# First layer: a plain pause before the transposes of the next chunk's rows becomes a rest until the next scan step

## The chip, the core and the metric

The kernel runs as one program on one core of a Trainium2 chip, in float32 throughout. The metric is the device time of one execution in microseconds (us). TensorE is called PE here, VectorE DVE, ScalarE ACT, GpSimd POOL, and SP is the engine that issues most DMAs.

## The reference

Four blocks with residual sums run over `x` of 4 sequences of 2048 rows, 256 wide: a time-mixing block with a gated linear recurrence, a mixture of 2 shared and 16 routed experts (these two are the first layer of the kernel), a selective state-space block, and a dropless mixture of 2 x 32 experts. The part that matters here is the head of the first block:

```python
x = x + _L0_attn_ref(_layernorm(x), ...)
x = x + _L0_ffn_ref(_layernorm(x), ...)
...
def _L0_attn_ref(x, ...):
    h = rms_norm(x, ln1_w)
    xx = jnp.pad(h[:, :-1], ((0, 0), (1, 0), (0, 0))) - h
    xr = h + xx * mu_r            # likewise xk, xv, xw, xg
    r, k, v = xr @ Wr, xk @ Wk, xv @ Wv
    g = silu(xg @ Wg)
    decay = exp(-exp(w0 + tanh(xw @ wA) @ wB))
    # per head: o_t = r_t (S + u k_t v_t);  S = decay_t S + k_t v_t
    o = group_norm(o) * gn_w + gn_b
    x = x + (o * g) @ Wo
    x = x + gelu(rms_norm(x, ln2_w) @ ffn_w1) @ ffn_w2
```

## The kernel before, in words

The first layer (`layer0_phase`) takes the 8192 rows in 16 chunks of 512. Each chunk's recurrence is a scan of 32 steps, one per pair of a half of the channels (2) and a value column (16). In every step POOL multiplies keys and values (L876), DVE scans along time (L885) and multiplies the states by the receptance (L891), and every fourth step PE sums four products (L907).

All other work is written as Python generators that are advanced while the instructions of the scan are recorded, so a fixed order of instructions per engine comes out; each engine then runs its own list in order and waits on semaphores. In step `g`, `background.pull()` advances five streams, each by its rate: `before(c + 1)`, which prepares the next chunk, at 1.3 advances per step, the head norms at 1.5, `attention_out` and `expert_inputs` at 3. A stream's unused part of an advance is carried on, so at 1.3 a stream is advanced once in most steps and twice in every third or fourth one. After that `block_work` (the experts of chunk `c - 2` and the feed-forward of chunk `c - 1`) is advanced until PE has been given about 4800 columns in the step; what the streams put on PE counts in this sum. A `yield` ends an advance, so what stands behind it is recorded at the next advance, which may lie in the same step. `rest(steps)` yields until the step counter has moved on by so many steps, at most three times for each:

```python
            until = now[0] + steps
            for _ in range(3 * steps):
                if now[0] >= until:
                    break
                yield
```

`before(c)` goes: statistics of the rows `xa` (`normalise`, DVE and POOL), ACT scaling them into `ha` in two pairs of 128 rows with a `yield` between them (`scaled`, L359), then `transposed`: for each half of the channels four PE transposes into one PSUM bank (L369) and ACT moving that bank to `hT` (L377). Then come, each with its own yields, the mixes (DVE L428), decay (PE, ACT L475, L477), keys and receptance (ACT L441), values (ACT L501), and the gate (PE, ACT L517, DVE L520), and the bonus (PE with `of_head`, DVE L530). The PE results of all these streams, of W_up of the experts and of the feed-forward's first product go into a ring of three PSUM banks, `G`; `claim` takes the next bank that is not held, and the matmul waits until the one who read it last is done.

Others named below: the head norm (`head_norm`) is a PE matmul with `centre`, a square on ACT (L553), a PE matmul with `same_head`, then Ln and Exp on ACT (L561, L563), for which ACT loads another table (L559), and two DVE multiplies (L566, L569). The experts go W_up on PE, Gelu on ACT (L791), a multiply by the gate on POOL (L802) and W_down on PE (L783), which runs three experts behind W_up. The feed-forward does the same with `w1`, Gelu (L666) and `w2` (L658). The gates come from a router matmul on PE, a softmax and top-4 on ACT and DVE (up to L728), a PE transpose (L733), a copy on ACT (L741), and two DMAs that spread them. `experts_out` (DVE L815) adds an expert sum to the rows and so frees the two banks of W_down.

Steps are counted from 0 to 31 in the scan of the chunk before the one that is prepared.

Of the kernel before, what the change touches and what calls it, by code (L numbers as in the profile page):

```python
# [210 lines left out]
def layer0_phase(nc, psum, consts, I, L, sems, x_in, x_out, second_layer):  # L211
# [6 lines left out]
    with ExitStack() as st, ExitStack() as scanning:  # L218
# [92 lines left out]
        def rest(steps):  # L311
# [6 lines that stand above are left out]
# [33 lines left out]
        def scaled(dst, src, scale, bias):  # L351

            for t in range(TL):
                if t == TL // 2:
                    yield
                if bias is None:
                    m = act.mark(nc.scalar.activation(dst[:, t, :], src[:, t, :], ACT.Copy, scale=scale[:, t:t + 1]))
                else:
                    m = act.mark(nc.scalar.activation(dst[:, t, :], src[:, t, :], ACT.Identity, scale=scale[:, t:t + 1], bias=bias[:, t:t + 1]))  # L359
            return m  # L360
# [33 lines left out]
        def before(c):  # L394
# [15 lines left out]
            yield  # L410
            act.after(m, m_done.get(("mixed", c - 1)))
            m = m_done["xa free", c] = yield from scaled(ha, xa, roots[:, TL:], shift[0])
            yield
            act.after(m_halo)
            marks = yield from transposed(ha, lambda kb: hT[:, kb, 1:C + 1], m, lambda kb: cols["ln1_w"][:, kb:kb + 1])
            yield
# [515 lines left out]
        def stages(c):  # L932

            def prepare():
                main, chain, inputs, ahead = [], [], [], [first] if c == 0 else []
                if c >= 1:
                    main.append(block_work(c - 2 if c >= 2 else None, c - 1))
                    chain.append(attention_out(c - 1))
                    inputs.append(expert_inputs(c - 1))
                if c + 1 < NCH:  # L940
                    ahead.append(before(c + 1))
                return main, chain, inputs, ahead, [head_norm(c, 0)]
            return prepare

        last = NCH - 1

        first = before(0)
        Background((1, [first])).drain(until=lambda: is_done(("ready", 0)))
        load_xa(1)
# [1136 lines left out]
```

How the kernel before makes its waits and increments, by code:

```python
    def after(self, *marks):  # L49
        for m in marks:
            if m is None or m.body != self.body or self.waited.get(m.lane, 0) >= m.ordinal:
                continue
            self.waited[m.lane] = m.ordinal
            self.engine.wait_ge(m.lane.sem, m.lane.base + m.ordinal)
# [6 lines left out]
    def finish(self):  # L63
        assert self.count < LANE_STEP
        if self.count:
            self.engine.wait_ge(self.sem, self.base + self.count)
        self.engine.sem_inc(self.sem, LANE_STEP - self.count)
# [14 lines left out]
    def begin(self, index):  # L83
        self.bodies += 1
        for lane in self.all:
            lane.begin(index * LANE_STEP + 1, self.bodies)
        for lane in self.all:
            for other in self.all:
                if other is not lane:
                    lane.engine.wait_ge(other.sem, other.base)
        self.sp.engine.sem_inc(self.sp.pause, 1)
# [117 lines left out]
def layer0_phase(nc, psum, consts, I, L, sems, x_in, x_out, second_layer):  # L211
# [77 lines left out]
        dve.mark(nc.vector.memset(carry[:, :], 0.0))  # L289
        dve.mark(nc.vector.memset(hT[:, :, C], 0.0))
        dve.mark(nc.vector.memset(kv[:, :, 0], 0.0))
        for i in range(2):
            m_first = dve.mark(nc.vector.memset(decay[i][:, :, 0], 1.0))
        dve.engine.wait_ge(s_load, loaded_first)
        dve.after(m_first)
        dve.mark(nc.vector.tensor_scalar(col_pack[:, len(A_COLS):, :], col_pack[:, len(A_COLS):, :], 0.5, None, ALU.mult))
```

## Time and profile before

| | |
|---|---|
| median of 3 runs | 4985.46 us (4985.34 to 4995.43) |
| profiled execution, its own time | 4976.51 us |
| its span from the first to the last instruction | 4974.7 us |
| mean granted TensorE clock | 0.935 |
| busy: PE, DVE, POOL, ACT | 88%, 77%, 61%, 51% |

The first layer takes about the first 2200 us of the span. A busy PE is not PE at its peak, and the sum of busy times of one engine says little on which engine makes the others wait; that is read from the waits and from the engines' instructions in order of time.

### The profile page before, as it was taken

To read this page: it belongs to the slowest core of one execution; us is meant where nothing else is said; L and a number is where in the kernel's file an instruction comes from. 1 tells how busy PE (TensorE), PEld (TensorE's weight loads), DVE (VectorE), ACT (ScalarE), POOL (GpSimd) and SP (SyncE) were. 2 spreads that over 40 slices of the span, in tenths; PEclk is the share of its full clock that TensorE was granted. 3 is DMA by queue.
4 is the path that set the end of the run, shared out by engine and by line. 5 is a ranking of instruction groups with operands and counts; after the bars stand their busy time and mean duration, and the time that the engine had idled before them with its cause. 6 is when DMAs were issued, how large, how long until landed. Compare 5 with 4: busy or idle time off the path is not lost.

```text
span 4974.7 us, 58244 instructions
## 1 busy us (share of the span) xinstructions
PE 4357.1 (88%) x18832; PEld 2868.4 (58%) x18832; DVE 3827.0 (77%) x6152; ACT 2521.3 (51%) x4753; POOL 3045.1 (61%) x1956
## 2 busy tenths in 40 slices
PE   5789999999999999998988889998988888489994
PEld 1355555555555555565655655555555555378883
DVE  6897888878777887884168888888888888645677
ACT  1244333433433343333567777777777776245552
POOL 3455554545545455553167888888888888745552
PEclk7899999999999999999989999999999998699997
DMA  4233332333333233332121121112221111486787
GB/s 143 80 106 107 104 102 85 109 106 102 106 104 104 84 108 106 98 110 84 45 85 55 71 71 64 64 65 74 77 84 65 70 65 61 162 240 205 255 279 279
DMA packets 302509, 545.46 MB, mean 110 GB/s; under 512 B 30592, under 2 KB 146560, under 8 KB 293248
## 3 DMA queue, kind: packets, MB, share of 16 engines
q1 hardware_dynamic: 274560, 466.08, 29.0%
q0 software_dynamic: 27648, 75.67, 4.2%
q8 instruction: 153, 2.51, 0.2%
q14 instruction: 148, 1.21, 0.1%
HBM read 422.71 MB, written 118.92 MB: 109 GB/s over the span
## 4 chain that ended last, share of the span: by engine, by line
PE 59%; DVE 18%; ACT 10%; POOL 6%; issue 4%; DMA 2%; SPq 0%; DVEq 0%; another core or an unknown queue 0%; POOLq 0%; ACTq 0%
PE psum L207 23%; PE psum L783 8%; PE psum L1891 5%; DVE c_hs L1426 5%; PE psum L658 5%; POOL c_dbx L1408 4%; PE psum L1150 4%; PE psum L1442 3%; DVE a_S L885 3%; PE psum L1914 3%; PE psum L1198 3%; DVE a_prod L891 2%; PE psum L907 2%; ACT psum L1415 2%; PE psum L1876 1%
## 5 line engine op out<-in xcount | busy, mean ns | idle before, releaser
L1408 POOL TENSOR_TENSOR c_dbx<-c_dtx,c_Brep 128x1024 f32<-128x1024 f32 x512 | 1203.0, 2365 | 266.6 <-DVE c_hs L1426 211.3
L876 POOL TENSOR_TENSOR a_kv<-a_rk,a_kv 128x512 f32<-128x512 f32 x512 | 813.5, 1601 | 387.4 <-DMA a_kv<-v_rows 387.4
L1426 DVE TENSOR_TENSOR_SCAN c_hs<-psum,c_carry,c_dbx 128x512 f32<-128x512 f32 x768 | 934.8, 1264 | 148.7 <-ACT psum L1415 115.9
L802 POOL TENSOR_TENSOR a_hid_e<-a_hid_e,a_g_rep 128x512 f32<-128x512 f32 x256 | 386.8, 1513 | 823.8 <-ACT a_hid_e L791 646.9
L885 DVE TENSOR_TENSOR_SCAN a_S<-a_decay,a_carry,a_kv 128x513 f32<-128x513 f32 x512 | 792.0, 1547 | 103.0 <-POOL a_kv L876 99.0
L1415 ACT ACTIVATE psum<-c_dt,c_cols 128x512 f32<-128x512 f32 x1024 | 694.1, 687 | 296.7 <-DVE c_hs L1426 288.1
L1442 PE MATMUL psum<-ident,c_hs 128*128 128x128 f32 x4096 | 656.6, 299 | 152.8 <-DVE c_hs L1426 146.5
L1442 PEld LDWEIGHTS psum<-ident,c_hs 128*128 128x128 f32 x4096 | 521.7, 153 | 410.5 <-DVE c_hs L1426 239.8
L891 DVE TENSOR_TENSOR a_prod<-a_rk,a_S 128x512 f32<-128x512 f32 x512 | 580.9, 1135 | 78.8 <-PE psum L907 78.8
L783 PE MATMUL psum<-a_W_down,a_hid_e 128*128 128x256 f32 x2304 | 550.9, 385 | 62.1 <-DVE a_carry L883 35.5
L207 PE MATMUL psum<-a_xT,a_W_up 128*128 128x512 f32 x1152 | 561.1, 617 | 26.2 <-ACT a_hid_e L791 15.2
L783 PEld LDWEIGHTS psum<-a_W_down,a_hid_e 128*128 128x128 f32 x2304 | 436.0, 192 | 226.6 <-issue 79.8
L1804 POOL DMA_INDIRECT results<-d_ys,d_to_row x320 | 312.0, 975 | 241.5 <-issue 145.3
L207 PEld LDWEIGHTS psum<-a_xT,a_W_up 128*128 128x128 f32 x1152 | 217.6, 195 | 268.5 <-issue 208.5
L1426 DVE TENSOR_TENSOR_SCAN c_hs<-psum,c_dbx 128x512 f32<-128x512 f32 x256 | 296.6, 1207 | 68.3 <-ACT psum L1415 49.8
L791 ACT ACTIVATE a_hid_e<-psum 128x512 f32<-128x512 f32 x288 | 171.1, 594 | 323.6 <-PE psum L207 322.9
L1891 PE MATMUL psum<-d_w,d_xT 128*128 x1280 | 331.3, 382 | 0.4 <-ACT d_xT L1879 0.2
L1365 POOL DMA_INDIRECT sorted_rows<-route_xn,route_to_row x256 | 263.0, 1027 | 64.8 <-issue 46.9
L1198 PE MATMUL psum<-c_xs,c_W_dt 128*128 128x512 f32 x512 | 255.5, 625 | 23.6 <-ACT c_dt L1223 21.0
L207 PE MATMUL psum<-a_xT,a_w 128*128 128x256 f32 x1024 | 240.8, 384 | 10.9 <-ACT a_decay L475 7.8
L658 PE MATMUL psum<-a_w,a_hid_f 128*128 128x256 f32 x1024 | 244.6, 382 | 1.5 <-ACT a_hid_f L666 0.3
L1150 PE MATMUL psum<-c_pre,c_taps 128*128 128x512 f32 x512 | 242.5, 596 | 0.5 <-ACT c_pre L1143 0.4
(263 smaller groups left out, 6890.9 us busy)
## 6 DMA issues: line engine op xcount, KB each, us to landing
a_kv<-v_rows SPq DMA_DIRECT2D x512, 256.0 KB
a_g_rep<-g_rows SPq DMA_DIRECT2D x256, 256.0 KB, 4.0
c_Brep<-b_rows SPq DMA_DIRECT2D x64, 1024.0 KB
d_xs<-sorted_rows SPq DMA_DIRECT2D x320, 128.5 KB
d_w<-results SPq DMA_DIRECT2D x64, 512.0 KB, 11.4
d_w<-in_d_experts SPq DMA_DIRECT2D x32, 768.0 KB
sorted_rows<-d_zeros SPq DMA_DIRECT2D x66, 128.5 KB, 11.3
a_xa<-in_L_attn_x SPq DMA_DIRECT2D x16, 512.0 KB, 4.6
```

The lines of the kernel that those rows point to most:

```text
L207: last = nc.tensor.matmul(out, lhsT, rhs, start=(n == 0), stop=(n == len(pairs) - 1))
L658: m_down = nc.tensor.matmul(sums[:, t * D:(t + 1) * D], hid_f[:, r, s * HALF + t * P:s * HALF + (t + 1) * P], w2[:, 2 * (f - 1) + s, :], s ...
L783: m_down = nc.tensor.matmul(banks[t // 2][1][:, (t % 2) * D:(t % 2 + 1) * D], hid_e[:, r, t * P:(t + 1) * P], W_down[:, q, :], start=(q == ...
L876: m_kv[g] = pool.mark(nc.gpsimd.tensor_tensor(kv[:, g % NV, 1:C + 1], rk[slot][:, 1, hb, :], kv[:, g % NV, 1:C + 1], ALU.mult))
L885: m_scan[q] = dve.mark(nc.vector.tensor_tensor_scan(S[:, q % NS, :], decay[cq % 2][:, hb, :], kv[:, q % NV, :], carry[:, sq_:sq_ + 1], ALU ...
L891: m_prod[q] = dve.mark(nc.vector.tensor_tensor(prod[:, q % NP, :], rk[cq % 2][:, 0, sq_ // DK, :], S[:, q % NS, 0:C], ALU.mult))
L1150: m = nc.tensor.matmul(bank, taps[:, e, j, :], pre[:, e, j:j + C], start=(j == 0), stop=(j == KC - 1))
L1408: m_dbx[g] = m_dbx[g + 1] = pool.mark(nc.gpsimd.tensor_tensor(dbx[:, r:r + 2, :], dtx[slot][:, e, :].unsqueeze(1).broadcast_to([P, 2, C]), ...
L1415: m_da[g] = act.mark(nc.scalar.activation(psum[:, DA + g % ND, :], dt[slot][:, e, :], ACT.Exp, scale=A[:, e, n:n + 1]))
L1426: m_scan[q] = dve.mark(nc.vector.tensor_tensor_scan(hs[:, q % NR, :], psum[:, DA + q % ND, :], dbx[:, q % NX, :], first, ALU.mult, ALU.add))
L1442: last = nc.tensor.matmul(psum[:, YB + e % 2, t * P:(t + 1) * P], hs[:, q % NR, t * P:(t + 1) * P], ident[:, :], is_transpose=True, start= ...
L1891: m = nc.tensor.matmul(bank[:, 0:2 * P], xT[:, q % N3, kb * P:(kb + 1) * P], w[:, bass.ds(at_w[q] + kb * 2 * P, 2 * P)], start=(kb == 0), ...
```

## The change

The pause between the last scaling by ACT and the first transpose is a rest of one step in place of a plain yield.

```diff
@@ -410,7 +410,7 @@
             yield
             act.after(m, m_done.get(("mixed", c - 1)))
             m = m_done["xa free", c] = yield from scaled(ha, xa, roots[:, TL:], shift[0])
-            yield
+            yield from rest(1)
             act.after(m_halo)
             marks = yield from transposed(ha, lambda kb: hT[:, kb, 1:C + 1], m, lambda kb: cols["ln1_w"][:, kb:kb + 1])
             yield
```

The numbers of instructions stay the same on every engine; their order changes, and more than the one line shows, since every later yield of `before(c)`, the columns given to `block_work`, and the phase in which the stream enters the next chunk move with it. In the order of before, chunks 3 to 15 are all alike: scaling in steps 5 and 6, transposes in steps 6 and 7. In the changed order they come in two kinds that alternate. For odd chunks (3, 5 to 15) the scaling stays in steps 5 and 6, the transposes come in steps 7 and 8, and the last instruction of `before` moves from step 29 to step 31. For even chunks (4 to 14) the scaling comes in steps 4 and 5 and the transposes stay in steps 6 and 7. Three places show it.

The first is PE around the transposes of chunk 7 (`a_ha` are its scaled rows, `a_sq` is the head norm's square). Before:

```order
L783 MATMUL psum<-a_W_down,a_hid_e 128x256 x4
L207 MATMUL psum<-a_sq,a_same_head 128x512
L369 MATMUL psum<-ident,a_ha 128x128 x4
L207 MATMUL psum<-a_xT,a_W_up 128x512 x2
L907 MATMUL psum<-a_prod,a_to_value 32x512 x4
L369 MATMUL psum<-ident,a_ha 128x128 x4
```

and now:

```order
L207 MATMUL psum<-a_sq,a_same_head 128x512
L783 MATMUL psum<-a_W_down,a_hid_e 128x256 x4
L207 MATMUL psum<-a_xT,a_W_up 128x512 x2
L907 MATMUL psum<-a_prod,a_to_value 32x512 x4
L369 MATMUL psum<-ident,a_ha 128x128 x4
L783 MATMUL psum<-a_W_down,a_hid_e 128x256 x4
```

The first transposes stood right behind the matmul with `same_head`; now a W_down, a W_up and the scan's sums stand between.

The second is a place that the diff does not mention: the head norm of the first half of the channels, in steps 20 to 24, and what PE and ACT have around it. PE before, around the second values matmul (`a_Wv`):

```order
L207 MATMUL psum<-a_xm,a_Wv 128x512 x2
L658 MATMUL psum<-a_w,a_hid_f 128x256 x4
L907 MATMUL psum<-a_prod,a_to_value 32x512 x4
L207 MATMUL psum<-a_sq,a_same_head 128x512
L783 MATMUL psum<-a_W_down,a_hid_e 128x256 x4
L207 MATMUL psum<-a_xT,a_W_up 128x512 x2
L207 MATMUL psum<-a_xm,a_Wg 128x512 x2
```

PE now, for an odd chunk (first fence) and for an even one:

```order
L207 MATMUL psum<-a_xm,a_Wv 128x512 x2
L207 MATMUL psum<-a_sq,a_same_head 128x512
L658 MATMUL psum<-a_w,a_hid_f 128x256 x4
L207 MATMUL psum<-a_xT,a_W_up 128x512 x2
L783 MATMUL psum<-a_W_down,a_hid_e 128x256 x4
L207 MATMUL psum<-a_xm,a_Wg 128x512 x2
```

```order
L207 MATMUL psum<-a_xm,a_Wg 128x512 x2
L207 MATMUL psum<-a_sq,a_same_head 128x512
L783 MATMUL psum<-a_W_down,a_hid_e 128x256 x4
L207 MATMUL psum<-a_xT,a_W_up 128x512 x2
L207 MATMUL psum<-a_xm,a_Wg 128x512 x2
L783 MATMUL psum<-a_W_down,a_hid_e 128x256 x4
```

ACT now, for the same odd chunk and the same even one:

```order
L501 COPY a_rv<-psum 128x512 x2
L559 ACT_TABLE_LOAD
L561 ACTIVATE a_sq<-psum,eps 128x512
L563 ACTIVATE a_sq<-a_sq 128x512
L666 ACT_TABLE_LOAD
L666 ACTIVATE a_hid_f<-psum 128x512
L791 ACTIVATE a_hid_e<-psum 128x512 x2
L517 ACTIVATE a_gate<-psum 128x512
```

```order
L561 ACTIVATE a_sq<-psum,eps 128x512
L563 ACTIVATE a_sq<-a_sq 128x512
L517 ACT_TABLE_LOAD
L517 ACTIVATE a_gate<-psum 128x512
L791 ACT_TABLE_LOAD
L791 ACTIVATE a_hid_e<-psum 128x512 x2
```

For the odd chunk `same_head` stands right behind the values matmul and `w2` right behind `same_head`, while the last Gelu of the feed-forward (L666) has moved behind Ln and Exp on ACT. For the even chunk the first gate matmul stands ahead of `same_head`, the tanh of the gate (L517) stands between Exp and the Gelu (L791), and a second table load stands between tanh and Gelu.

The third is PE at the start of a chunk, from the router matmul on. Before:

```order
L207 MATMUL psum<-a_W_router,a_xT 128x16 x8
L907 MATMUL psum<-a_prod,a_to_value 32x512 x4
L207 MATMUL psum<-a_xT,a_W_up 128x512 x8
L783 MATMUL psum<-a_W_down,a_hid_e 128x256 x4
L733 MATMUL psum<-ident,a_gates 16x128 x4
L207 MATMUL psum<-a_xT,a_W_up 128x512 x2
L783 MATMUL psum<-a_W_down,a_hid_e 128x256 x4
L207 MATMUL psum<-a_xT,a_W_up 128x512 x2
L783 MATMUL psum<-a_W_down,a_hid_e 128x256 x4
```

and now:

```order
L207 MATMUL psum<-a_W_router,a_xT 128x16 x8
L783 MATMUL psum<-a_W_down,a_hid_e 128x256 x4
L207 MATMUL psum<-a_xT,a_W_up 128x512 x8
L907 MATMUL psum<-a_prod,a_to_value 32x512 x4
L733 MATMUL psum<-ident,a_gates 16x128 x4
L783 MATMUL psum<-a_W_down,a_hid_e 128x256 x4
L207 MATMUL psum<-a_xT,a_W_up 128x512 x2
L783 MATMUL psum<-a_W_down,a_hid_e 128x256 x4
L207 MATMUL psum<-a_xT,a_W_up 128x512 x2
L783 MATMUL psum<-a_W_down,a_hid_e 128x256 x4
```

The last W_down of the previous chunk's experts comes behind the router, and the transposes of the gates come ahead of the first W_down of the next experts and not behind it.

## Rows read from the trace of the kernel before

**Rows 1.** busy time in one chunk of layer 0: length, PE, PEld, DVE, ACT, POOL, clock, DMA.

```profile
746.24:889.19 142.95, 133.81 (x520) 82.93 (x520) 118.74 (x146) 55.50 (x92) 76.30 (x49) 0.99 0.31 102
```

**Rows 2.** waits of PE over layer 0: total us, times, longest.

```profile
PE psum L369 <- ACT a_ha L359: 47.6, 15, 13.7
PE psum L783 <- DVE a_carry L883: 35.5, 13, 3.1
...
PE psum L783 <- POOL a_hid_e L802: 26.6, 15, 2.2
```

**Rows 3.** PE in order of time, near 746 us: start, length, instruction, [idle before].

```profile
742.70 1.02 PE L207 MATMUL psum<-a_sq,a_same_head 128*128 128x512 f32 x2
746.24 0.63 PE L369 MATMUL psum<-ident,a_ha 128*128 128x128 f32 x4 [2.51 <-ACT a_ha L359]
748.05 3.36 PE L207 MATMUL psum<-a_xT,a_W_up 128*128 128x512 f32 x4 [1.19 <-ACT a_hid_e L791]
```

**Rows 4.** ACT in order of time, the same place.

```profile
743.76 0.69 ACT L561 ACTIVATE a_sq<-psum,eps 128x512 f32<-128x512 f32 x1 [0.94 <-PE psum L207]
744.48 0.63 ACT L563 ACTIVATE a_sq<-a_sq 128x512 f32<-128x512 f32 x1
745.01 1.08 ACT L359 ACTIVATE a_ha<-a_xa,a_shift,a_roots 128x256 f32<-128x256 f32 x2
746.11 1.28 ACT L791 ACT_TABLE_LOAD   x1
```

**Rows 5.** PE in order of time, from a chunk's last router matmul into the next chunk.

```profile
850.27 1.85 PE L207 MATMUL psum<-a_W_router,a_xT 128*128 128x16 f32 x16
852.06 1.06 PE L907 MATMUL psum<-a_prod,a_to_value 128*32 128x512 f32 x8
853.05 7.13 PE L207 MATMUL psum<-a_xT,a_W_up 128*128 128x512 f32 x16
863.14 1.97 PE L783 MATMUL psum<-a_W_down,a_hid_e 128*128 128x256 f32 x8 [2.96 <-DVE a_carry L883]
...
872.44 1.99 PE L783 MATMUL psum<-a_W_down,a_hid_e 128*128 128x256 f32 x8 [1.73 <-POOL a_hid_e L802]
```

**Rows 6.** DVE in order of time, the same place.

```profile
861.58 0.22 DVE L728 TENSOR_TENSOR a_gates<-a_gates,a_router_total 128x64 f32<-128x64 f32 x1
861.72 1.28 DVE L815 TENSOR_TENSOR a_xb<-a_xb,psum 128x512 f32<-128x512 f32 x2
...
863.26 1.29 DVE L885 TENSOR_TENSOR_SCAN a_S<-a_decay,a_carry,a_kv 128x513 f32<-128x513 f32 x1
864.46 0.67 DVE L891 TENSOR_TENSOR a_prod<-a_rk,a_S 128x512 f32<-128x512 f32 x1
```

**Rows 7.** PE at the same place one chunk earlier.

```profile
717.20 3.17 PE L783 MATMUL psum<-a_W_down,a_hid_e 128*128 128x256 f32 x8 [3.11 <-DVE a_carry L883]
720.16 1.06 PE L733 MATMUL psum<-ident,a_gates 128*16 128x128 f32 x4
```

**Rows 8.** POOL in order of time, that earlier place.

```profile
727.17 2.49 POOL L802 TENSOR_TENSOR a_hid_e<-a_hid_e,a_g_rep 128x512 f32<-128x512 f32 x2 [12.65 <-ACT a_hid_e L791]
```

**Rows 9.** DVE in order of time, steps 20 and 21.

```profile
798.97 3.02 DVE L487 SCALAR_TENSOR_TENSOR a_xm<-a_rk,a_cols 128x512 f32<-128x512 f32 x2 [2.21 <-ACT a_rk L441]
801.91 1.40 DVE L428 SCALAR_TENSOR_TENSOR a_xm<-a_ha,a_cols,a_hT 128x512 f32<-128x512 f32 x2
803.23 0.68 DVE L674 TENSOR_TENSOR a_xb<-a_xb,psum 128x512 f32<-128x512 f32 x1
```

**Rows 10.** PE in order of time, from the head norm to the gate.

```profile
820.26 1.12 PE L207 MATMUL psum<-a_sq,a_same_head 128*128 128x512 f32 x2
...
834.32 1.98 PE L207 MATMUL psum<-a_xT,a_W_up 128*128 128x512 f32 x4 [0.71 <-DVE a_gate L520]
```

**Rows 11.** DVE in order of time, the same place.

```profile
817.65 1.41 DVE L428 SCALAR_TENSOR_TENSOR a_xm<-a_ha,a_cols,a_hT 128x512 f32<-128x512 f32 x2 [6.88 <-PE psum L207]
...
833.61 0.65 DVE L520 SCALAR_TENSOR_TENSOR a_gate<-a_gate,psum 128x512 f32<-128x512 f32 x1
```

## The prediction

> **What bounds the kernel now.** I first read the busy times of one steady chunk of the first layer. Of its 143 us PE is busy 134, DVE 119, POOL 76 and ACT 56, at a granted clock of 0.99 [rows 1]. So PE sets the pace, and a chunk gets shorter when PE waits less. Next I read what PE waits for over the layer [rows 2]. The largest entry is the transposes of the scaled rows waiting for ACT, 47.6 us in 15 waits. 13.7 us of it is one wait, at the start of the kernel, which the change doesn't touch. The others in the sum that follows are waits of W_down for DVE (35.5 us in 13) and for POOL (26.6 us in 15). Last I read the engines in order of time at the three places that the new order moves.
>
> **What the change takes away.** At the transposes, PE ends the `same_head` matmul at 743.72 and then waits 2.51 us [rows 3], because ACT still has Ln, Exp and two scalings to do (0.69, 0.63, 1.08) [rows 4]. Behind them come a table load of 1.28 and the Gelu that frees a bank for the next W_up, which so waits another 1.19 us [rows 3, 4]. The pair, 3.70 us, recurs in chunks 3 to 15, 13 x 3.70 = 48.1 us. In the new odd chunks a W_down, a W_up and the scan's sums stand before the transposes: 1.97 + 7.13/4 + 1.06 = 4.8 us [rows 5] against the 4.3 us from `same_head`'s end to the W_up that the Gelu releases [rows 3]. In the new even chunks the scaling is done a step before Ln and Exp. Both cover the whole 3.70, so I count 48.1 as gone.
>
> At the start of a chunk, router and softmax end in gates ready at 861.80, 9.7 us after the router matmul, and the two banks are free at 863.00, when the first W_down starts after 2.96 us of waiting [rows 5, 6]. The transposes of the gates come behind it. One chunk earlier they start at 720.16, and POOL has the spread gates 7.0 us later, at 727.17 [rows 7, 8]; the third W_down waits for that product, 1.73 us [rows 5] and 26.6/15 = 1.8 on average [rows 2]. In the new order DVE does the same work up to the gates, and the transposes start as soon as these are ready, about 10 us after the router. POOL can then start near 17 and has the first product near 18.3 (2.49/2 for one) [rows 8]; PE comes to the third W_down near 20. I take that wait as gone: 13 x 1.8 = 23.4 us. The first W_down now waits for DVE to free the banks behind one more scan and product (1.29 + 0.67) [rows 6], so 2.0 us later. But PE has one more W_down (1.97) and the transposes ahead of it. So I cost that wait at nothing; the cover is that W_down, and without it the price is 2.0 us a chunk. Taken away: 48.1 + 23.4 = 71.5 us.
>
> **What it adds.** The later steps of `before` move too, and the rotation of the three banks with them. Here the trace of before shows no such wait, so each is worked out from lengths of instructions.
>
> Odd chunks (7 of them). (a) PE's `centre` matmul stands two `w1` groups behind the scan's sums of step 19, about 3.5 us. DVE must do after the same sums a product (0.67), two multiplies of 3.02, two mixes of 1.40 and an addition of 0.68 [rows 6, 9], 5.8 us; the multiplies may take about 2.4 where POOL is idle. I take a wait of 2.0; the ends are 0 and 3.7. (b) `same_head` stands right behind the values matmul, in a bank that ACT frees by copying that very matmul's result, about 0.65 (an ACT pass over 128x512, as Exp) [rows 4]. Then `w2` needs a Gelu that has moved behind Ln and Exp: table load, Ln, Exp, table load, Gelu, 1.28 + 0.69 + 0.63 + 1.28 + 0.6 = 4.5 us from the copy's end [rows 4], of which PE fills 0.9 with `same_head`. So PE waits 0.65 + 3.6 = 4.25. DVE uses that time for the chain up to the gate, which took 834.26 - 817.65 = 16.6 us [rows 11], so the wait of 0.71 for the gate [rows 10] goes: net 3.5. (c) The second transpose group of the expert inputs reuses a bank that ACT has just to empty: 0.65. (d) ACT loads two more tables per chunk, 1.28 each [rows 4]; one lies in the chain to the transposes of the feed-forward's rows. I take 1.0, between 0 and 2.6. Sum 2.0 + 3.5 + 0.65 + 1.0 = 7.15 us a chunk, 50.0 us.
>
> Even chunks (6). (e) Behind `same_head` PE has one W_down (1.97) and then a W_up whose bank is freed by a Gelu behind Ln, Exp, table load, tanh, table load: 0.69 + 0.63 + 1.28 + 0.6 + 1.28 + 0.6 = 5.1 us [rows 4]. The wait is some 3.3; less the 0.71 that goes as above, 2.6 [rows 10]. In before the same Gelu came behind `same_head` with one table load only, and PE had W_down and W_up ahead. (f) Extra table loads in the chain to the feed-forward: 0.4, between 0 and 2.6. Sum 3.0 us, 18.0 us for six.
>
> Added: 68.0 us. **The sum** is 68.0 - 71.5 = -3.5 us. The profiled execution took 4976.5 us (span 4974.7), so 4973 for its like. The median of the runs shown is 9 us above it, so I forecast **4982 us** for the median: no change that a measurement could tell, which I set at 0.2%, or 10 us. The second layer, from about 2300 us on, is not touched.
>
> **A rule that speaks against it.** After a wait of 2.96 us the eight W_down matmuls took 1.97 us [rows 5]; after one of 3.11 us they took 3.17 [rows 7], as at TensorE's lower level, 1.2 GHz for 2.4. The Trainium skill, TensorE: Matmul & The Clock Gate, section "Why this matters for your kernels", asks for no long idle gaps between bursts of matmuls, since the clock then falls back. By that rule the new waits of (b) and (e) are worse than what they replace; these two rows agree that a gap of this size can cost clock. No other number here needs it.
>
> **The rivals.**
> 1. *The new waits cost half* (chance 0.25). DVE's multiplies in (a) run fast, the table loads in (d) and (f) end beside other PE work, and Gelu and bank come in time in part of the cases. For it: DVE had waits of 2.21 and 6.88 us of its own at these places [rows 9, 11], so it has room. Against: (b) and (e) are serial on ACT whatever DVE does. Then odd chunks add 0.65 + 3.5 = 4.15 or less, even ones 2.0: 29 + 12 = 41 us, and the sum is -30: 4955 us.
> 2. *The bank release at the start of a chunk decides* (0.17). If DVE reaches the gates late, the extra W_down doesn't cover the scan and product ahead of the release, PE waits 2.0 us more in 13 chunks, and the third W_down then keeps its wait of 1.8 because POOL too comes late. It decides from the point where the bank release falls more than 2.0 us later than now, counted from the router. For it: DVE had only 0.2 us between the banks' release and the next scan, so it was never idle here [rows 6]. Against: its work up to the gates is the same. The sum is -3.5 + 26 + 23.4 = +46 in full and +21 for half of it: 5007 to 5031; I put it at 5007, slower.
> 3. *The clock* (0.15). Each new wait of 3.3 to 3.6 us costs 3.17 - 1.97 = 1.2 us behind it [rows 5, 7], 13 x 1.2 = 15.6, less some 4 for the like of rows 7 that may go: +11, so -3.5 + 11 = +8: 4993 us, still inside 10.
> 4. *The change hardly does what it says* (0.03). In the even chunks the transposes stay in their step and it is the scaling that moves; were the wait to remain in these, 6 x 3.70 = 22 us of the gain would be gone: +19, 5004 us.
>
> **How the numbers follow.** The forecast case has 0.40. From it and the clock rival most lies within 10 us of before. Faster gets rival 1 and the lower end of the forecast, 0.28; slower gets rivals 2 and 4, and the upper ends of (a), (d) and the clock, 0.30; the same is left with 0.42. The likeliest case's own range is 4968 to 4996. To hold 8 in 10 it has to reach to rival 1 at the bottom and rival 2 at the top: 4952 to 5012.
>
> **What would show it.** Right: the transposes of the scaled rows and the W_up behind them have no wait but in the first two chunks; the wait of W_down for POOL goes, that for the bank release stays near 2.9; new waits stand before `centre` (about 2), before `w2` (3.6) in every second chunk, and before a W_up behind `same_head` (3.3) in the others; chunks alternate in length, odd ones about 1.7 us longer than now and even ones about 2.5 us shorter. Wrong: new waits of over 5 us there, or none; a wait of W_down for DVE near 5 us; a layer that is 25 us shorter or longer.

## The result and the profile after

The changed kernel takes 5079.34 us (median of 4 runs, 5070.96 to 5084.20), the kernel before 4985.40 in the same session: a ratio of 1.0185, interval 1.0163 to 1.0206. It is slower by 94 us; the forecast was 4982, with a range of 4952 to 5012. On PE, DVE and POOL the numbers of instructions are those of before. On ACT they are not: it ran 4776 for 4753, 23 more table loads.

The loss lies in the first layer. These two rows, one for each kernel, group the router matmuls by line and tile (count, ns shortest/median/longest, first and last start). Before:

```profile
L207 PE MATMUL psum<-a_W_router,a_xT x256: 179/263/376, 271.3 to 2416.3; 128*128 128x16 f32 x128
```

After:

```profile
L207 PE MATMUL psum<-a_W_router,a_xT x256: 179/263/283, 268.5 to 2504.0; 128*128 128x16 f32 x128
```

From the first chunk's router to the sixteenth's it was 2145.0 us and is 2235.5: 90.5 of the 94 us. I call this stretch the layer's length. Both kinds of chunk are longer. In order of time, three routers of PE after:

```profile
1191.03 1.96 PE L207 MATMUL psum<-a_W_router,a_xT 128*128 128x16 f32 x16
...
1341.47 1.96 PE L207 MATMUL psum<-a_W_router,a_xT 128*128 128x16 f32 x16
...
1491.33 1.96 PE L207 MATMUL psum<-a_W_router,a_xT 128*128 128x16 f32 x16
```

150.4 us for an odd chunk and 149.9 for an even one. Before, the router of [rows 5] and the two behind it stand at 850.27, 994.56 and 1139.98, so 144.9 on average.

The busy times over this stretch (columns as in [rows 1]) show the two halves of the loss. Before:

```profile
271.30:2416.30 2145.00, 1996.83 (x7721) 1246.29 (x7719) 1674.37 (x2094) 827.65 (x1368) 1101.67 (x703) 0.98 0.31 100
```

After:

```profile
268.50:2504.00 2235.50, 2039.63 (x7721) 1277.88 (x7720) 1599.40 (x2094) 857.75 (x1391) 1060.99 (x703) 0.96 0.30 96
```

PE's idle time rose from 148.2 to 195.9 us, by 47.7, and the same 7721 matmuls took 42.8 us longer, at a granted clock of 0.96 where it was 0.98. DVE and POOL got less busy, not more: 1674 to 1599 us and 1102 to 1061. So neither of them ran out of room; PE waits more, and runs slower when it doesn't wait.

What PE waits for over the layer. Before, beside [rows 2]:

```profile
PE psum L207 <- ACT a_hid_e L791: 15.2, 13, 1.2
...
PE psum L207 <- ACT a_lora L464: 7.3, 3, 5.8
...
PE psum L658 <- ACT a_hid_f L666: 0.3, 1, 0.3
```

After:

```profile
PE psum L207 <- ACT a_hid_e L791: 34.4, 10, 5.3
PE psum L783 <- DVE a_xb L815: 29.0, 12, 4.2
...
PE psum L207 <- ACT a_lora L464: 26.4, 9, 5.8
PE psum L658 <- ACT a_hid_f L666: 24.4, 8, 3.4
PE psum L207 <- DVE a_xa L604: 21.2, 13, 2.8
PE psum L733 <- DVE a_gates L728: 16.0, 12, 8.4
PE psum L207 <- DVE a_o L547: 15.0, 10, 8.1
PE psum L369 <- ACT a_ha L359: 14.7, 2, 13.6
```

The transposes' wait for the scaled rows is left in the first two chunks only (47.6 to 14.7 us), and that of W_down for POOL went from 26.6 to 4.2. In their place four have grown by some 20 us each: W_up for a Gelu (15.2 to 34.4), `wB` for a Tanh (7.3 to 26.4), `w2` for a Gelu (0.3 to 24.4), and `wA` for the addition of the attention's output, `a_xa` (none before, 21.2 now). `wA` doesn't use that sum; the bank of the ring that it takes was last read by this addition. The waits for the gates and before `centre` (9.4 and 9.8 before) grew by 6.6 and 5.2.

The waits of an odd chunk in PE's order of time (two of 0.34 and 0.60 us at `wB` and the first `w1`, which before has too, are left out):

```profile
1246.42 2.96 PE L207 MATMUL psum<-a_xm,a_wA 128*64 128x512 f32 x4 [2.83 <-DVE a_xa L604]
...
1256.22 1.10 PE L369 MATMUL psum<-ident,a_hb 128*128 128x128 f32 x8 [0.85 <-ACT a_hid_e L791]
...
1287.93 1.13 PE L207 MATMUL psum<-a_o,a_centre 128*128 128x512 f32 x2 [0.55 <-DVE a_o L547]
...
1302.99 1.13 PE L207 MATMUL psum<-a_sq,a_same_head 128*128 128x512 f32 x2 [0.67 <-ACT a_rv L501]
1307.56 3.78 PE L658 MATMUL psum<-a_w,a_hid_f 128*128 128x256 f32 x8 [3.44 <-ACT a_hid_f L666]
...
1335.57 0.66 PE L369 MATMUL psum<-ident,a_hb 128*128 128x128 f32 x4 [0.68 <-ACT a_xT L375]
...
1353.96 0.60 PE L733 MATMUL psum<-ident,a_gates 128*16 128x128 f32 x4 [0.85 <-DVE a_gates L728]
1356.93 3.39 PE L783 MATMUL psum<-a_W_down,a_hid_e 128*128 128x256 f32 x8 [2.38 <-DVE a_xb L815]
```

And of an even one (but for one of 1.01 at the first `w1`, where before waits 0.94 in two):

```profile
1390.66 1.93 PE L207 MATMUL psum<-a_xm,a_wA 128*64 128x512 f32 x4 [0.77 <-DVE a_xa L604]
...
1398.63 1.95 PE L207 MATMUL psum<-a_lora,a_wB 64*128 64x512 f32 x4 [3.12 <-ACT a_lora L464]
1400.51 3.55 PE L207 MATMUL psum<-a_xT,a_W_up 128*128 128x512 f32 x4
...
1415.60 1.98 PE L207 MATMUL psum<-a_xm,a_Wk 128*128 128x512 f32 x4 [0.68 <-ACT a_rk L441]
...
1428.57 1.99 PE L207 MATMUL psum<-a_xT,a_w 128*128 128x256 f32 x8 [1.18 <-ACT a_hid_f L666]
...
1462.34 3.61 PE L207 MATMUL psum<-a_xT,a_W_up 128*128 128x512 f32 x4 [3.53 <-ACT a_hid_e L791]
...
1503.37 0.60 PE L733 MATMUL psum<-ident,a_gates 128*16 128x128 f32 x4 [0.40 <-DVE a_gates L728]
1506.35 3.51 PE L783 MATMUL psum<-a_W_down,a_hid_e 128*128 128x256 f32 x8 [2.38 <-DVE a_xb L815]
```

Read the second column too. Eight matmuls of `w2` or W_down, or four of W_up, take 1.9 to 2.0 us at full clock [rows 5] (the rows count each matmul of the order twice, a transpose once). Behind the long waits they take 3.4 to 3.8, as at the lower level, 1.2 GHz for 2.4. The granted clock over the `w2` group, from 1307.56 to 1311.30, is 0.50, over the other slow groups 0.54 to 0.63, and over the W_down group of [rows 5] it is 1.00. Six groups of a pair are slow in this way: 1.0 (wA, 2.96 for 1.93), 1.9 (`w2`), 1.4 and 1.5 (W_down), 1.7 and 1.7 (W_up) too long, 9 us together.

Not every pair is like this one: wA waits 1.33 to 2.83 us in the odd chunks, and is slow in three of seven. And before had slow groups too. Its W_up behind the transposes took 2.83 to 3.78 us in all 13 chunks ([rows 3] shows one), its first W_down 1.97 us in one chunk and 2.74 to 3.17 in the next, in turn [rows 5, 7]. So the loss by slower matmuls, net, is the 42.8 us above and not 9 us for each pair.

Where the wait of `wB` comes from is seen on ACT, in order of time at that place:

```profile
1391.30 0.42 ACT L613 ACTIVATE a_hb<-a_xa 128x256 f32<-128x256 f32 x1 [4.21 <-DVE a_xa L604]
...
1392.82 0.18 ACT L613 ACTIVATION_READ_ACCUMULATOR a_hb<-a_xa 128x1 f32 x1
1393.02 1.28 ACT L340 ACT_TABLE_LOAD   x1
1394.31 0.30 ACT L342 ACTIVATE a_ms<-a_ssq,a_eps_rms 128x4 f32<-128x4 f32 x1
...
1394.88 1.71 ACT L357 ACTIVATE a_hb<-a_xa,a_ms 128x256 f32<-128x256 f32 x4
1396.60 1.28 ACT L464 ACT_TABLE_LOAD   x1
1397.90 0.59 ACT L464 ACTIVATE a_lora<-psum 64x512 f32<-64x512 f32 x1
```

ACT idles 4.2 us for DVE's addition of the attention's output, then does the statistics and the scaling for the feed-forward, and only behind these, and a table load, the Tanh that `wB` waits for. DVE, at the same time:

```profile
1386.40 2.00 DVE L885 TENSOR_TENSOR_SCAN a_S<-a_decay,a_carry,a_kv 128x513 f32<-128x513 f32 x1
1388.32 1.68 DVE L891 TENSOR_TENSOR a_prod<-a_rk,a_S 128x512 f32<-128x512 f32 x1
1389.93 1.27 DVE L604 TENSOR_TENSOR a_xa<-a_xa,psum 128x512 f32<-128x512 f32 x2
```

The addition stands behind a scan and a product, and these took 2.00 and 1.68 us here against 1.29 and 0.67 in [rows 6].

### The profile page after: what moved, and what is told of

Read it like the earlier page. It is cut to its first block, busy times and chain, and to the rows that moved or that the text cites. A ratio compares the mean times of both kernels' runs of the same rounds, so it can differ in the third digit from the quotient of the medians.

```text
span 5069.2 us, 58247 instructions
## 1 busy us (share of the span) xinstructions
PE 4399.5 (87%) x18832; PEld 2899.1 (57%) x18832; DVE 3754.5 (74%) x6152; ACT 2549.4 (50%) x4776; POOL 2997.6 (59%) x1956
## 3 DMA queue, kind: packets, MB, share of 16 engines
q8 instruction: 153, 2.51, 0.2%
## 4 chain that ended last, share of the span: by engine, by line
PE 55%; DVE 19%; ACT 10%; POOL 8%; issue 6%; DMA 1%; SPq 0%; DVEq 0%; POOLq 0%; another core or an unknown queue 0%; ACTq 0%
PE psum L207 22%; PE psum L783 7%; POOL c_dbx L1408 5%; PE psum L1891 5%; PE psum L658 4%; DVE c_hs L1426 4%; PE psum L1150 3%; DVE a_S L885 3%; PE psum L1198 3%; PE psum L1914 3%; PE psum L1442 3%; DVE a_prod L891 2%; PE psum L907 2%; ACT psum L1415 2%; POOL sorted_rows L1365 1%
## 5 line engine op out<-in xcount | busy, mean ns | idle before, releaser
L876 POOL TENSOR_TENSOR a_kv<-a_rk,a_kv 128x512 f32<-128x512 f32 x512 | 778.3, 1532 | 425.8 <-DMA a_kv<-v_rows 425.5
L802 POOL TENSOR_TENSOR a_hid_e<-a_hid_e,a_g_rep 128x512 f32<-128x512 f32 x256 | 375.8, 1471 | 914.3 <-ACT a_hid_e L791 674.4
L891 DVE TENSOR_TENSOR a_prod<-a_rk,a_S 128x512 f32<-128x512 f32 x512 | 530.4, 1036 | 129.0 <-PE psum L907 129.0
L783 PE MATMUL psum<-a_W_down,a_hid_e 128*128 128x256 f32 x2304 | 568.9, 393 | 33.3 <-DVE a_xb L815 29.0
L207 PE MATMUL psum<-a_xT,a_W_up 128*128 128x512 f32 x1152 | 562.0, 618 | 34.4 <-ACT a_hid_e L791 34.4
L783 PEld LDWEIGHTS psum<-a_W_down,a_hid_e 128*128 128x128 f32 x2304 | 450.3, 198 | 205.9 <-issue 101.7
L791 ACT ACTIVATE a_hid_e<-psum 128x512 f32<-128x512 f32 x288 | 169.8, 595 | 429.9 <-PE psum L207 429.0
L658 PE MATMUL psum<-a_w,a_hid_f 128*128 128x256 f32 x1024 | 253.5, 395 | 24.7 <-ACT a_hid_f L666 24.4
L658 PEld LDWEIGHTS psum<-a_w,a_hid_f 128*128 128x128 f32 x1024 | 200.5, 198 | 90.0 <-ACT a_hid_f L666 32.5
```

Source lines behind the costliest of these rows:

```text
L207: last = nc.tensor.matmul(out, lhsT, rhs, start=(n == 0), stop=(n == len(pairs) - 1))
L658: m_down = nc.tensor.matmul(sums[:, t * D:(t + 1) * D], hid_f[:, r, s * HALF + t * P:s * HALF + (t + 1) * P], w2[:, 2 * (f - 1) + s, :], s ...
L783: m_down = nc.tensor.matmul(banks[t // 2][1][:, (t % 2) * D:(t % 2 + 1) * D], hid_e[:, r, t * P:(t + 1) * P], W_down[:, q, :], start=(q == ...
L876: m_kv[g] = pool.mark(nc.gpsimd.tensor_tensor(kv[:, g % NV, 1:C + 1], rk[slot][:, 1, hb, :], kv[:, g % NV, 1:C + 1], ALU.mult))
L891: m_prod[q] = dve.mark(nc.vector.tensor_tensor(prod[:, q % NP, :], rk[cq % 2][:, 0, sq_ // DK, :], S[:, q % NS, 0:C], ALU.mult))
```

## The experiments

Layer length is worked out as above. The kernel before took 4985.4 us beside the change, 4983.5 beside the next four rows, 4990.0 beside the four after these and 4993.5 beside the last three; so a difference of a few us between rows is read from the ratio or from the layer, not from the medians.

| run | median us | ratio to before (interval) | layer length us |
|---|---|---|---|
| the change | 5079.34 | 1.0185 (1.0163 to 1.0206) | 2235.5 |
| all chunks odd | 5079.48 | 1.0188 (1.0171 to 1.0205) | 2244.2 |
| all chunks even | 5184.91 | 1.0403 (1.0386 to 1.0421) | 2345.4 |
| transposes catch up | 5136.30 | 1.0302 (1.0285 to 1.0319) | 2303.6 |
| scaling in one step | 4950.46 | 0.9930 (0.9913 to 0.9947) | 2119.1 |
| all odd, norm later | 5021.43 | 1.0063 (1.0047 to 1.0078) | 2186.6 |
| all odd, kept busy | 5017.88 | 1.0056 (1.0041 to 1.0071) | 2187.9 |
| one step, kept busy | 4952.84 | 0.9927 (0.9914 to 0.9941) | 2117.6 |
| table ahead | 5067.78 | 1.0161 (1.0146 to 1.0177) | 2226.0 |
| the change, kept busy | 5044.31 | 1.0111 (1.0095 to 1.0127) | 2190.5 |
| one step, two fills | 4948.87 | 0.9915 (0.9901 to 0.9928) | 2112.8 |
| all odd, both repairs | 4979.01 | 0.9972 (0.9963 to 0.9982) | 2142.2 |

The theory (A) is that the loss is PE's new waits behind ACT and DVE, with the slower matmuls behind each. Its rivals: the alternation of two kinds of chunk (B), the odd kind alone (C), the later transposes as such (D), DVE or POOL as the bound (E). Rivals F to H stand in the expectations of the runs that they concern.

**All chunks odd.** The change, with the stream's carried-over part of an advance set to the same value at each chunk:

```diff
                         background.drain(until=lambda: is_done(("ready", c)))
+                    background.streams[3][1] = 1.0
                     for stream, stages in zip(background.streams, chunks[j][1]()):
```

> The change with the stream of the next chunk given the same credit (1.0) at every chunk's start, so that all chunks are of the odd kind. Theory A (the new waits of PE behind ScalarE and VectorE, each with slower matmuls behind it, are the loss, in both kinds alike): about 5.5 to 8 us a chunk over before, 5055 to 5095 us. Rival B (it is the switching between two kinds from chunk to chunk that costs; each kind alone is about as fast as before): 4970 to 5000. Rival C (the odd kind alone carries the loss): 5120 to 5170.

Measured 5079, like the change itself. Alternation is not needed for the loss, so B falls.

**All chunks even.** The same line with 0.6.

> The change with credit 0.6 at every chunk's start: all chunks of the even kind, in which the transposes stay in their step and the scaling is a step earlier. Theory A: 5055 to 5095 us, with the wait of about 3.5 us of W_up behind the same_head matmul in every chunk. Rival B: 4970 to 5000. Rival C (the odd kind carries the loss): 4970 to 5000 here and far over 5100 with all odd.

Measured 5185, the worst of all, so C falls as well. A is missed too, by 90 us. The waits of this kind grew where every chunk has them; two rows of PE in one chunk:

```profile
1205.58 3.78 PE L207 MATMUL psum<-a_xT,a_W_up 128*128 128x512 f32 x4 [5.26 <-ACT a_hid_e L791]
...
1250.68 3.75 PE L783 MATMUL psum<-a_W_down,a_hid_e 128*128 128x256 f32 x8 [4.20 <-DVE a_xb L815]
```

In the even chunks of the change these two were 3.53 and 2.38. The wait of W_down for POOL, which the change had taken away, is back here (26.8 us over the layer). Why the waits grow so when even chunks follow each other is not shown.

**Transposes catch up.** The change, without the pause behind the transposes, so that what follows stands a step earlier:

```diff
             marks = yield from transposed(ha, lambda kb: hT[:, kb, 1:C + 1], m, lambda kb: cols["ln1_w"][:, kb:kb + 1])
-            yield
             m_xx = []
```

> The change with the yield behind the moves to hT taken out, so that the transposes stay one step later in every chunk while the later steps of the preparation end in step 29 as before, and all chunks are alike. Theory A (moving the transposes is good by itself, the loss is in the later steps that moved with them): the waits at the transposes are gone and the w2 wait of 3.4 us too; 4940 to 4985 us. Rival D (transposes a step later are themselves the loss, since mixes and decay come closer to their users): 5040 to 5090.

Measured 5136, over both ranges, and A's forecast for this form, that the time comes back with the later steps, is wrong. There are new waits again, on mixes that DVE now has too little time for and on Gelus, with slow groups behind them:

```profile
1252.56 3.35 PE L207 MATMUL psum<-a_xm,a_wA 128*64 128x512 f32 x4 [5.62 <-DVE a_xm L427]
...
1276.46 3.42 PE L207 MATMUL psum<-a_xT,a_W_up 128*128 128x512 f32 x4 [5.00 <-ACT a_hid_e L790]
```

The first row is D's own mechanism, so this run doesn't exclude D. What speaks against D as the cause in the change is that PE's waits for the mixes `a_xm` are 26.7 us there over the layer and 25.9 before, against 95.2 in this form.

**Scaling in one step.** The kernel before, with the transposes where they were and the scaling no longer split over two advances:

```diff
-                if t == TL // 2:
+                if pause and t == TL // 2:
                     yield
...
-            m = m_done["xa free", c] = yield from scaled(ha, xa, roots[:, TL:], shift[0])
+            m = m_done["xa free", c] = yield from scaled(ha, xa, roots[:, TL:], shift[0], False)
```

> The kernel before, with its plain yield, but ScalarE scales all four parts in one advance, a step ahead of Ln and Exp; later steps stay where they are. Theory A: the wait of 2.51 us at the transposes goes in 13 chunks and most of the 1.19 behind it: 4937 to 4955 us. Rival E (PE's waits there cover others, VectorE or GpSimd take over the pace): 4975 to 4995.

Measured 4950, inside A's numbers, and faster than both kernels. It removes most of the same wait of the transposes as the change does (0.39 and 0.58 us are left of 2.51 and 1.19) and the slow W_up behind it (1.98 for 3.36 [rows 3]), but leaves the later work in its steps. So taking that wait away was worth 33 us, net of a wait that is new here as well: wA waits for `a_xa`, 20.7 us in 14. What the change lost, it lost elsewhere.

**All odd, norm later.** The all-odd form, with ACT's Ln and Exp of one half recorded two steps later, behind the Gelu that `w2` waits for:

```diff
+            if kb == 0:
+                yield from rest(2)
             nc.scalar.preload_act_table_set("natural_log_exp_and_others")
```

> The all-odd form of the change (5079 us before this edit), with one difference: ScalarE records Ln and Exp of the first half of the head norm two steps later, so that the last feed-forward Gelu stands ahead of them. TensorE's order is the same. Theory A (the loss is TensorE's waits behind ScalarE and VectorE, and the slower matmuls behind each): the wait of w2 for a_hid_f, 3.45 us in each of 13 chunks, and some 1.5 us of slower w2 matmuls behind it go, 13 x 4.95 = 64 us, so 5005 to 5030, w2 at 1.9 to 2.0 us in place of 3.4. Rival E (TensorE is only as early as VectorE lets it be, so a wait taken out comes back at the next bank or sum): 5060 to 5085, with the W_down wait for VectorE grown from 2.4 to over 4 us.

Measured 5021, 58 us less: A's number. The `w2` groups are back at 1.89 us without a wait. One of the all-odd form, then one of this run:

```profile
1296.84 3.42 PE L658 MATMUL psum<-a_w,a_hid_f 128*128 128x256 f32 x8 [3.45 <-ACT a_hid_f L666]
```

```profile
1428.70 1.89 PE L660 MATMUL psum<-a_w,a_hid_f 128*128 128x256 f32 x8
```

Of the 45.2 us that the all-odd form waits at `w2` little came back elsewhere: 9.7 us in ten waits of the gate matmul for `a_gate` are new, and the waits for a Gelu before the transposes of `hb`, 22.5 us in the all-odd form, are 25.8. The W_down wait for DVE stayed at 2.38, so E falls for this wait.

**All odd, kept busy.** The all-odd form, with matmuls of a zero matrix `idle` meant for three of PE's waits; they add zero to running sums or write a bank that is idle. `fill(n, ...)` issues n of them, and no wait is taken out:

```diff
+                fill(6, FD.tensor[:, FD.first, 0:D], w2[:, 0, :], True)
             pe.after(m)
             m = xm_free[0] = pe.mark(matmuls(nc, bank[0:LORA, :]
...
+                        if half == 1 and f == FB // 2:
+                            fill(7, sums[:, 0:D], w2[:, 0, :], False)
                         pe.after(hid[r])
...
+                            fill(5, FD.tensor[:, FD.first, 0:D], w2[:, 0, :], True)
                         banks = [EB.take(pe) for _ in range(2)]
```

> The all-odd form of the change (5079 us before this edit), with added matmuls of a zero matrix that fill three waits of TensorE in each chunk from the second on: 7 ahead of the last w2 (they add zero to its sums), 6 ahead of wA, 5 ahead of the first W_down (into an idle bank). What TensorE waits for is not changed. Theory A with the clock (the matmuls behind a wait run at the lower level, 3.4 us for 1.9): three groups a chunk are 1.2 to 1.8 us shorter and 13 chunks give 45 to 70 us, so 5010 to 5035, with a granted clock of 0.97 or more in the steady chunks in place of 0.94. Rival F (slower matmuls are hidden by the same late ScalarE and VectorE, so the clock costs nothing of the end time): 5070 to 5095.

Measured 5018, 62 us less, though no wait was removed and work was added. The two rows of PE at `w2`, and the busy times of a stretch of the layer (columns as in [rows 1]), with a clock of 1.00:

```profile
1275.20 3.19 PE L387 MATMUL psum<-a_w,a_idle 128*128 128x256 f32 x14
1278.81 1.99 PE L670 MATMUL psum<-a_w,a_hid_f 128*128 128x256 f32 x8 [0.42 <-ACT a_hid_f L678]
```

```profile
1200.00:1600.00 400.00, 382.62 (x1510) 245.26 (x1510) 307.61 (x379) 162.33 (x263) 194.65 (x130) 1.00 0.31 98
```

The slower matmuls lay on the path that sets the end; rival F falls for this kernel. But the 62 us are not the price of the clock alone, since one of the three places is not filled. PE claims the ring's bank ahead of the fills for wA, so that these stand behind the wait and not in it:

```profile
1217.60 2.86 PE L387 MATMUL psum<-a_w,a_idle 128*128 128x256 f32 x12 [1.91 <-DVE a_xa L614]
```

Over 13 chunks these fills took 44.8 us; the waits before the transposes of `hb` that follow, 22.5 us in the all-odd form, went in exchange.

**One step, kept busy.** The kernel with the scaling in one step, and 6 such matmuls ahead of the first W_down of a chunk, as in the last piece above.

> The kernel before with the scaling recorded in one step (4950 us), with 6 matmuls of a zero matrix into an idle bank ahead of the first W_down of each chunk, where TensorE waits 2.97 us and the W_down group behind takes 3.48 us. Theory A with the clock: 1.0 to 1.5 us a chunk in 13 chunks, 13 to 20 us, so 4930 to 4940. Rival F: 4948 to 4960.

Measured 4953 for 4950: no gain that a median shows, which is F's number and misses A's. The rows tell more. Without the fill, first and third W_down of a chunk:

```profile
1272.90 3.48 PE L783 MATMUL psum<-a_W_down,a_hid_e 128*128 128x256 f32 x8 [2.97 <-DVE a_carry L883]
...
1283.89 1.99 PE L783 MATMUL psum<-a_W_down,a_hid_e 128*128 128x256 f32 x8 [1.91 <-POOL a_hid_e L802]
```

With it:

```profile
1270.29 1.97 PE L793 MATMUL psum<-a_W_down,a_hid_e 128*128 128x256 f32 x8 [0.38 <-DVE a_carry L893]
...
1279.97 3.20 PE L793 MATMUL psum<-a_W_down,a_hid_e 128*128 128x256 f32 x8 [2.12 <-POOL a_hid_e L812]
```

In this chunk the slow group moved on to the next wait, that for POOL. This is so in five chunks (2.69 to 3.20 us), where without the fill ten first W_downs were slow. From the second router to the fourteenth a chunk is 0.7 us shorter than without the fill, some 8 us in all; but the first chunk and the last two, most of whose fills meet no wait, are 6.6 us longer. So the clock did cost end time in the steady part, less than A had it.

**Table ahead.** The change, with the table of Tanh and Gelu loaded ahead of the two waits behind which a Tanh stands:

```diff
+            nc.scalar.preload_act_table_set("gelu_and_others")
             m_lora = G.freed[i] = act.mark(nc.scalar.activation(lora[:, :], bank[0:LORA, :], ACT.Tanh))
...
+                nc.scalar.preload_act_table_set("gelu_and_others")
                 m = act.mark(nc.scalar.activation(gate[slot][:, ob, :], bank, ACT.Tanh, scale=0.5))
```

> The change itself (5079 us), with ScalarE told to load the Gelu and Tanh table ahead of the wait for the low-rank product and ahead of the wait for the gate product, where the load of 1.28 us stood between the matmul and its Tanh. Theory A: up to 1.28 us off the wait of wB for a_lora (2.6 us x 9 chunks) and off the waits behind the gate's Tanh (W_up in even chunks, hbT in odd ones), 13 to 30 us in all, so 5045 to 5065. Rival E: 5072 to 5085.

Measured 5068, 12 us less (9.5 by the layer), just over A's range and below E's. The waits of W_up for a Gelu fell from 34.4 to 25.7 us over the layer, but the one aimed at first did not: `wB` waited 30.4 us in 9 for 26.4. At `wB` the table load is not what decides.

**The change, kept busy.** The change itself, with the zero matmuls at the long waits of each kind of chunk (4 ahead of wA and 7 ahead of the last `w2` in odd ones; 6 ahead of `wB` and 7 ahead of the W_up in even ones, shown; 5 ahead of the first W_down in both):

```diff
+                if e == 13 and c % 2 == 1:
+                    for k in range(7):
+                        nc.tensor.matmul(banks[0][1][:, 0:D], idle[:, :], W_down[:, 0, :], start=False, stop=False, skip_group_check=True)
                 if e < NE:
                     i, bank = yield from G.claim(pe)
```

> The change itself (5079 us), with added matmuls of a zero matrix in the new waits, and nothing else altered: in every odd chunk 4 ahead of wA and 7 ahead of the last w2, in every even one 6 ahead of wB and 7 ahead of the W_up behind same_head, in both 5 ahead of the first W_down. What TensorE waits for is the same. Theory A with the clock: of the +94 us the waits are some 35 and the slower matmuls some 60; a pair of chunks has six slowed groups, together about 9 us, so 6.5 x 9 = 58 us less: 5010 to 5035, clock 0.99 in the steady chunks. Rival F (the slower matmuls are hidden): 5070 to 5095. Rival G (the clock is all of the loss): 4980 to 4995.

Measured 5044: 35 us less by the medians, 43 if each is taken against before in its own session, 45 of the 90.5 by the layer's length. That is less than A's 58. The fills ahead of wA again stand behind its wait; in the seven odd chunks they took 14.5 us. Even without these it would be far from G's 4980 to 4995, so both F and G fall: a part of the loss is the clock, but not all of it. Part of the time won at full clock was waited for again. In an even chunk, where the fill removed the slow group before it, wA now waits 2.43 us where it waited 0.77 (13.9 us over the six even chunks, for 6.6):

```profile
1360.76 3.57 PE L207 MATMUL psum<-a_xm,a_wA 128*64 128x512 f32 x4 [2.43 <-DVE a_xa L617]
```

**One step, two fills.** The one-step kernel with 6 fills ahead of the first and 4 ahead of the third W_down.

> The kernel before with the scaling in one step and 6 zero matmuls ahead of the first W_down of a chunk (4953 us), with 4 more ahead of the third W_down, which waits 2.1 us for GpSimd and whose group took 3.20 us once the first no longer ran slowly. Theory A with the clock: the slow groups behind that wait, 1.2 + 0.4 us in 13 chunks, go: 4928 to 4940. Rival H (the slow matmuls move on to the next wait once more, wA's of 1.4 us): 4945 to 4960 with wA or the group behind it above 3 us.

Measured 4949, and in a stretch of the layer the clock is 1.00. No slow group is left at the two waits, and the part of H that names one at wA or behind it falls, but its time holds: the layer is 5 us shorter than with one fill, and the intervals of this run, of one fill and of none overlap. From the second router to the fourteenth the chunk is 141.8 us, against 142.4 with one fill and 143.1 with none, so some 15 us over twelve chunks, of which more than half is lost again in the first chunk and the last two. Whether it is faster than the one-step kernel alone is not settled.

**All odd, both repairs.** The norm later, and fills ahead of wA (4) and the first W_down (5).

> The all-odd form with both repairs: Ln and Exp of the first half two steps later (5021 us alone) and the zero matmuls ahead of wA (4) and of the first W_down (5), of the three groups that gave 5018 us together. Theory A: the two remaining slow groups, 1.0 to 1.5 us each in 13 chunks, so 4980 to 4998, no slower than before by more than 0.2%. Rival E (another engine is by then the bound): 5010 to 5025.

Measured 4979, a microsecond under A's range: 100 us less than the all-odd form, and 0.3% under the kernel before. The order of the odd chunks loses nothing against before once ACT's Gelu stands ahead of Ln and Exp and PE is kept at its full clock (1.00 from 800 to 2000 us). Before itself was not run with such matmuls in its own waits, so this doesn't say that the order is as good.

## Why the prediction was wrong

What was to be removed, was: the 3.70 us at the transposes in 13 chunks, and the wait of the third W_down for POOL. The one-step kernel shows that the first of these was worth having. What failed is the other side of the sum, "Added: 68.0 us", and with it the -3.5 us: measured are 47.7 us more of waiting, net, and 42.8 us of slower matmuls.

The steps that it names for what is added mostly hold, in size and place: (b) 0.67 before `same_head` and 3.44 before `w2` for 0.65 and 3.6; (c) 0.68 for 0.65; (e) 3.53 for 3.3, though the lengths that (e) names give 3.1. For (d), the transposes of the feed-forward's rows wait 0.85 us in the odd chunk, for a Gelu behind one more table load than in before; the forecast was 1.0. The wait for the gate that was set off against (b) and (e) went (15.8 us in 14 before, one of 4.6 now). The bank-release wait stayed, at 2.38, as the text said. Term (a) was too large (0.55 for 2.0): DVE's two multiplies ahead of that `centre` took 1.41 us, where the prediction had 3.02, or 2.4 with POOL idle. Its upper end of 3.7 doesn't follow from its figures either, since 5.8 less 3.5 is 2.3.

Three things failed.

*The list of new waits was not complete.* The sentence for (f), "Extra table loads in the chain to the feed-forward: 0.4", took the chain of wA, Tanh and `wB` as otherwise unchanged. It measured 0.77 at wA and 3.12 at `wB` in the even chunk, and 2.83 at wA in the odd one, which had no term at all. PE, no longer held up at the transposes, comes to wA earlier, while DVE's addition of the attention's output still stands behind a scan and a product of full length. Before had no wait at wA; its wait at the transposes, it seems, gave DVE that time: the one-step kernel, which loses the same wait with all else in place, waits up to 1.40 us at wA in the steady chunks. Small waits of 0.4 to 1.2 us (transposes of the gates, keys, `w1`) were missed too. Together the missed waits are 3.7 us in the odd chunk (2.83 + 0.85) and 6.2 in the even one (0.77 + 3.12 + 0.68 + 1.18 + 0.40).

*The clock was sized as a side matter.* The sum has no term for it. Rival 3 had the right mechanism at 1.2 us behind each of 13 waits, 11 us net. Measured are 42.8 us, nearly half of the loss; with the fills, 45 of the layer's 90.5 us go, and in the all-odd form 56, both net of what the fills themselves took. The rule that the prediction set against the change (the Trainium skill, TensorE: Matmul & The Clock Gate, "Why this matters for your kernels": no long idle gaps between bursts of matmuls, since the clock falls back) holds here in direction, by these runs. Its price was to be read from rows like [rows 7], once for each new wait of 2.4 us and more, and for the bank release too, of which the prediction says "So I cost that wait at nothing": in before the group behind it was slow in every second chunk (1.97 [rows 5], 3.17 [rows 7]), after in nine on end (3.39 to 3.75). The prediction also left out a slow group that would go, the W_up of 3.36 us in [rows 3].

*Removed and added time were netted as if each wait stood alone.* By the form that kept the order, removing the wait at the transposes gave 33 us, not 48, though the slow W_up behind it went as well; and the lost time is spread over places whose waits feed each other. By the same token the terms found above do not add up in the pair shown: for the odd chunk the 1.7 that was forecast, 3.7 of waits and 4.3 of slow groups, less 1.6 for (a) and (d), is 8.1; for the even one -2.5 + 6.2 + 4.9 is 8.6. Before's own slow groups lie in its 144.9 us, 1.9 us a chunk on average (W_up 1.4, first W_down 0.5). Less these, 6.2 and 6.7 are left, an estimate from one pair, where 5.5 and 5.0 were measured. Slow groups shorten the next wait, as the change kept busy shows.

What stays open: whether wA's wait could be had for less. The scan and the product on DVE took 2.00 and 1.68 us there. POOL ran without a gap from 1384.73 to 1390.96, over both. Of the same instructions during which POOL was idle, between 300 and 2400 us, none took more than 1.29 (218 scans) and 0.69 (199 products); where POOL ran throughout, the medians were 2.23 and 1.68. So the trace sets the long ones beside POOL's work, but no run separates the two.

## What to carry to other kernels

A wait that you remove on the engine that sets the pace was also time for the others: list every place downstream where that engine will now be early, and look there for who is late, before you net anything. Prefer the edit that makes the late work earlier (here the scaling in one step, 0.7% faster) to one that puts the waiting work later, because the latter moves everything behind it past other queues. Price each remaining wait of TensorE together with the matmuls behind it; where a wait can't be removed, harmless matmuls in it can win back a part. See in the trace that they lie in the wait and not behind it, and that they are left out where there is none.

## What the hardware showed that was not expected

- Added matmuls made a kernel faster: 18 zero matmuls a chunk took the all-odd form from 5079 to 5018 us, with the granted clock from 0.95 to 1.00 between 1200 and 1600 us, although 6 of the 18 stood behind their wait.
- The slow group is not tied to one wait. With the first wait of a chunk filled, the group behind the second went from 1.99 to 3.20 us, behind a wait that was much the same (1.91 and 2.12), in five chunks of one run. And after 2.96 us of waiting eight W_down matmuls took 1.97 us [rows 5], after 2.38 us 3.39: the length of a wait alone does not tell. In before the first W_down was slow in every second chunk, behind waits that were alike (2.77 to 3.13 us).
- A table load on ACT cost 1.28 us and the next activation began within 0.02 us of its end (1393.02, 1.28, 1394.31). The Trainium skill, ScalarE: Activation LUTs, "What ACT_TABLE_LOAD costs", adds a drain of about 1.38 us to each switch; the row in front, which ended at 1393.00, leaves no room for one here.
